# The mixing's two diagonal blocks as 64-row matmuls into two banks, with the work around it reordered

## The reference, cut to what matters

```python
# x: (32, 64, 1024); two layers, each: x = x + ffn(cond(x, c))
def L0_cond(x, c, weight, c_weight, bias):      # grouped conv, 4 groups, 9 taps, + context per (n, o)
    out = conv_general_dilated(x, weight, padding=[(4, 4)], feature_group_count=4)
    return out + (c @ c_weight.T)[:, :, None] + bias[None, :, None]
def L0_ffn(x, weight, bias, lora_A, lora_B, starts):   # x @ weight.T (1024 x 1024) + bias + adapter of rank 16
    ...
def L1_cond(x, emb, W0, b0, W1, b1, W2, b2, weight, bias_k):
    h = gelu(emb @ W0 + b0); h = gelu(h @ W1 + b1); att = softmax(h @ W2 + b2)   # (32, 8)
    agg_w = einsum('bk,koi->boi', att, weight[..., 0])                            # one 64 x 64 per batch row
    agg_b = att @ bias_k
    return einsum('boi,bih->boh', agg_w, x) + agg_b[:, :, None]                   # "the mixing"
def L1_ffn(x, A, B, Wr):                          # 64 adapters of rank 16, 16 of them chosen per token
    scores = xf @ Wr.T; top_vals, top_idx = top_k(scores, 16); gates = softmax(top_vals)
    h = einsum('nd,krd->nkr', xf, A)              # 1024 x 1024
    return 2.0 * einsum('nkr,kdr->nd', h * G[:, :, None], B)                      # 1024 x 1024
```

## Time and profile before

| what | us |
|---|---|
| median of three runs | 669.21 |
| the profiled execution's own time | 671.31 |
| its span, first to last instruction | 669.5 |
| PE busy | 651.7 |
| PEld busy | 538.4 |
| DVE busy | 451.1 |
| ACT busy | 213.1 |
| POOL busy | 73.2 |

### The profile page before, as it was taken

One profiled execution on the slowest core, in us unless ns is written; L12 is line 12 of the kernel. 1 busy time (PEld: TensorE's weight loads), 2 busy tenths in 40 slices (PEclk: granted clock), 3 DMA queues, 4 the chain that ended last, 5 costly groups with the idle time before them and its releaser, 6 DMA issues.

```text
span 669.5 us, 8350 instructions
## 1 busy us (share of the span) xinstructions
PE 651.7 (97%) x3197; PEld 538.4 (80%) x3197; DVE 451.1 (67%) x688; ACT 213.1 (32%) x275; POOL 73.2 (11%) x91
## 2 busy tenths in 40 slices
PE   9999999997999999999999999999899999999996
PEld 7878888886897787887789788888689888888775
DVE  2859469549377788658669648636867847656864
ACT  2714134224134115335114312334323321333510
POOL 1499200000000070000000042000000000000000
PEclk9999999998999999999999999999999999999999
DMA  8577715976968836776985682374987664047684
GB/s 306 189 293 277 288 48 160 353 218 216 381 222 317 349 148 253 261 233 234 338 305 186 273 314 94 107 225 157 348 316 266 270 258 162 0 140 206 227 318 182
DMA packets 51450, 157.98 MB, mean 236 GB/s; under 512 B 5472, under 2 KB 6368, under 8 KB 51424
## 3 DMA queue, kind: packets, MB, share of 16 engines
q1 hardware_dynamic: 46096, 148.05, 60.6%
q10 hardware_dynamic: 5328, 9.61, 4.7%
HBM read 131.94 MB, written 25.71 MB: 235 GB/s over the span
## 4 chain that ended last, share of the span: by engine, by line
PE 59%; DMA 19%; DVE 14%; issue 3%; ACT 3%; ACTq 1%; SPq 0%; DVEq 0%
PE bank L1349 14%; PE bank L1351 13%; PE bank L1350 13%; DMA gate_x<-gates 12%; PE bank L1363 8%; DMA piece_lo<-kept 4%; PE bank L1383 3%; DMA raw<-pieces 3%; DVE piece_lo L882 2%; PE bank L1370 2%; ACT piece_hi L639 2%; DVE work L977 1%; DVE x L914 1%; DMA toep<-taps 1%; PE bank L1375 1%
## 5 line engine op out<-in xcount | busy, mean ns | idle before, releaser
L882 DVE TENSOR_TENSOR piece_lo<-raw,piece_hi 128x1024 fp32r<-128x1024 f32 x60 | 74.1, 1240 | 89.9 <-ACT piece_hi L639 89.7
L1349 PE MATMUL bank<-piece_hi,u_hi 128*128 128x512 f32 x272 | 109.0, 401 | 8.1 <-DVE piece_lo L882 4.6
L639 ACT ACTIVATE piece_hi<-raw 128x1024 fp32r<-128x1024 f32 x60 | 63.3, 1057 | 155.0 <-PE bank L1351 110.6
L1350 PE MATMUL bank<-piece_lo,u_hi 128*128 128x512 f32 x272 | 107.9, 397 | 0.0
L1351 PE MATMUL bank<-piece_hi,u_lo 128*128 128x512 f32 x272 | 107.8, 396 | 0.0
L1349 PE MATMUL bank<-v_hi,piece_hi 128*128 128x512 f32 x256 | 101.8, 398 | 0.0
L1351 PE MATMUL bank<-v_hi,piece_lo 128*128 128x512 f32 x256 | 101.1, 395 | 0.0
L1350 PE MATMUL bank<-v_lo,piece_hi 128*128 128x512 f32 x256 | 101.0, 394 | 0.0
L1349 PE MATMUL bank<-piece_hi,v_hi 128*128 128x512 f32 x192 | 76.2, 397 | 1.3 <-DMA piece_lo<-kept 1.3
L1351 PE MATMUL bank<-piece_hi,v_lo 128*128 128x512 f32 x192 | 75.8, 395 | 0.0
L1350 PE MATMUL bank<-piece_lo,v_hi 128*128 128x512 f32 x192 | 75.7, 394 | 0.0
(11 more groups left out here) (143 smaller groups left out, 800.2 us busy)
## 6 DMA issues: line engine op xcount, KB each, us to landing
raw<-pieces SPq DMA_DIRECT2D x76, 512.0 KB, 5.3
piece_hi<-kept SPq DMA_DIRECT2D x48, 512.0 KB, 4.9
piece_lo<-kept SPq DMA_DIRECT2D x48, 512.0 KB, 5.8
conv_in<-conv_x SPq DMA_DIRECT2D x16, 516.0 KB, 6.9
x<-x SPq DMA_DIRECT2D x16, 512.0 KB, 5.3
gate_x<-gates ACTq DMA_DIRECT2D x32, 256.0 KB
out<-x SPq DMA_DIRECT2D x32, 256.0 KB, 4.6
conv_in<-pieces SPq DMA_DIRECT2D x12, 512.0 KB, 8.7
```

What stands on the lines that cost most here:

```text
L639: act.activation(piece_hi[:, n % SLOTS, :], raw[:, r % RAWS, :], ACT.Copy).then_inc(s_piece_hi, 1)
L882: dve.tensor_tensor(piece_lo[:, n % SLOTS, :], raw[:, r % RAWS, :], piece_hi[:, n % SLOTS, :].bitcast(F32), ALU.subtract).then_inc(s_piece ...
L1349: pe.matmul(to, left_hi, right_hi, start=first, stop=False)
L1350: pe.matmul(to, left_hi, right_lo, start=False, stop=False)
```

## The change

It does eight things.

1. `mix` makes two matmuls per tile in place of one: partitions 0 to 63 with the first diagonal block, 64 to 127 with the second, 64 moving columns each. The first goes to bank `first`, the second to bank `first + 1`, in columns `t * 64` on. So a chunk has eight matmuls of 64 rows, and fills half of each of two banks. All banks are now one tensor, so that `mix_item` reads both halves in one instruction.
2. `LAG` goes from 3 to 2; the mixes use two pairs of banks (2 and 3, 5 and 6 in group 0; 6 and 7, 3 and 4 later). `h` of chunk 1 moves to bank 1 and the transposed scores to bank 0.
3. In groups 1 to 3 the mixes 0 and 1 are issued ahead of the last quarter of `winograd(12, ...)`, and on DVE their items and low parts ahead of four `x1` adds. The adds of banks 4 and 5 go ahead of those of 6 and 7.
4. In group 1 the splits of combined unit 3 leave the mixing: two go ahead of `choose`, two behind `split_raw(g, 17)`; SP's `keep_weights(3, ...)` and `load_conv_in` move later with them.
5. In group 0 `split_first(20)` and `split_first(21)` go into the middle of `combine(2)` and its splits.
6. `split_raw(g, 25)` goes ahead of `sums(4)`.
7. In the last group the `partial` of the last product is added into `x1` ahead of time, and its banks 1 and 0 are added straight into `x1`; the stores' counts follow.
8. `score_transposed` and the waits are renumbered to match.

```diff
-LAG = 3
+LAG = 2
-        H_BANKS = (2, 3, 6, 7, 4, 5, 2, 3)
+        H_BANKS = (2, 1, 6, 7, 4, 5, 2, 3)
+        FIRST_MIX_BANKS = (2, 5)
+        MIX_BANKS = (6, 3)
...
-            def mix(c, bank):
+            def mix(c, first):
                 for t in range(NT):
-                    mm = pe.matmul(banks[bank][:, t * P:(t + 1) * P], x1[:, t, c * P:(c + 1) * P],
-                                   blockdiag[:, t, :], start=True, stop=True)
+                    for b in range(2):
+                        rows = slice(b * C, (b + 1) * C)
+                        mm = pe.matmul(bank[:, first + b, t * C:(t + 1) * C], x1[rows, t, c * P:(c + 1) * P],
+                                       blockdiag[rows, t, rows], start=True, stop=True)
                 mm.then_inc(s_mix, 1)
...
-                winograd(12, (1, 0), u_hi, u_lo, block_of(1, 1), False)
+                winograd(12, (1, 0), u_hi, u_lo, block_of(1, 1), False, range(3))
+                pe.wait_ge(s_bd, 2 * g + 2)
+                pe.wait_ge(s_f, g * 24 + 20)
+                for i in range(LAG):
+                    mix(CHUNKS[i], MIX_BANKS[i])
+                winograd(12, (1, 0), u_hi, u_lo, block_of(1, 1), False, range(3, 4))
...
@@ DVE, group 0
-                combine(2)
-                for step in range(4):
-                    combined_lo(2, step)
-                for n in range(20, 23):
-                    split_first(n)
+                combine(2, 0)
+                split_first(20)
+                combine(2, 1)
+                combined_lo(2, 0)
+                combined_lo(2, 1)
+                split_first(21)
+                combined_lo(2, 2)
+                combined_lo(2, 3)
+                split_first(22)
...
@@ DVE, groups 1 to 3, at the mixing
+                for i in range(2):
+                    mix_item(g, i, CHUNKS[i], MIX_BANKS[i])
+                for i in range(2):
+                    mix_lo(g, i, CHUNKS[i])
+                for s in range(2):
+                    add(partial[:, s, :], 2 + s, 0, s_f)
+                for s in range(2):
+                    ffn_done(7 + s)
+                    read(s_f, 21 + s)
+                    add(banks[1 - s][:, :], 2 + s, 0, s_f)
+                for i in range(2, NCH):
+                    mix_item(g, i, CHUNKS[i], MIX_BANKS[i % 2])
+                    if i > 2:
                         mix_lo(g, i - 1, CHUNKS[i - 1])
-                    if g == 1 and i % 2:
-                        combined_lo(3, i // 2)
...
+                split_raw(g, 25)
                 dve.wait_ge(s_lo, g * ITEMS + ITEMS)
                 sums(4)
-                split_raw(g, 25)
...
+                if last:
+                    for s in range(2):
+                        for h in range(2):
+                            add(partial[:, s, :], 2 + s, h, s_o)
+                    for s in range(2):
+                        won(dve, g, 1, 6, s)
+                        for h in range(2):
+                            read(s_o, 17 + 2 * s + h)
+                            add(banks[1 - s][:, :], 2 + s, h, s_o)
```

More of the change, by code:

```diff
@@ L150, in adaln_ffn_kernel @@
         diag = x1[0:C, 2, 0:GB * C].rearrange("p (b c) -> p b c", b=GB)
-        banks = [ctx.enter_context(nc.psum_tensor(f"bank{i}", [P, HALF], F32)) for i in range(8)]
+        bank = ctx.enter_context(nc.psum_tensor("bank", [P, 8, HALF], F32))
+        banks = [bank[:, i, :] for i in range(8)]
         s_first = sem("s_first")
@@ L495, in group @@
                 next_raw(17)
-                if g == 1:
-                    for step in range(4):
-                        keep_weights(3, step)
-                elif not last:
+                if g > 1 and not last:
                     load_conv_in(g + 1, 0)
@@ L503, in group @@
                 if g == 1:
-                    load_conv_in(g + 1, 0)
-                    load_conv_in(g + 1, 1)
-                if not last:
+                    keep_weights(3, 0)
+                    keep_weights(3, 1)
+                elif not last:
                     load_conv_in(g + 1, 2)
                     load_conv_in(g + 1, 3)
-                for n in range(19, 22):
-                    next_raw(n)
+                next_raw(19)
+                if g == 1:
+                    keep_weights(3, 2)
+                    keep_weights(3, 3)
+                next_raw(20)
+                next_raw(21)
                 if not last:
@@ L515, in group @@
                 next_raw(23)
+                if g == 1:
+                    for t in range(NT):
+                        load_conv_in(g + 1, t)
                 if g == 1:
@@ L917, in add_partial, with mix_item @@
                 dve.tensor_tensor(partial[:, s, :], partial[:, s, :], banks[bank][:, :], ALU.add).then_inc(done, 1)
[L919 removed]
+            def mix_item(g, i, c, first):
                 dve.wait_ge(s_mix, g * NCH + i + 1)
[L921 to L922 removed]
+                dve.tensor_tensor(work[:, c, :].rearrange("p (t b c) -> p b t c", b=2, c=C),
+                                  bank[:, first:first + 2, 0:HALF // 2].rearrange("p b (t c) -> p b t c", c=C),
+                                  mixb_bc[:, :, :].rearrange("p (t b) c -> p b t c", b=2), ALU.add).then_inc(s_item, 1)
             def mix_lo(g, i, c):
@@ L1245, in group @@
                 for s in range(2):
-                    add(partial[:, s, :], 2 + s, 0, s_f)
+                    ffn_done(5 + s)
+                    read(s_f, 15 + s)
+                    add(banks[4 + s][:, :], 2 + s, 1, s_f)
                 for s in range(2):
@@ L1327, in group @@
                     split_raw(g, STEPS + 2)
[L1328 to L1333, removed]
+                if last:
[7 more added lines that the diff above has]
+                            add(banks[1 - s][:, :], 2 + s, h, s_o)
+                else:
+                    for s in range(2):
+                        won(dve, g, 1, 6, s)
+                        add_partial(1 - s, s, s_o)
+                        read(s_o, 17 + 3 * s)
+                        add(partial[:, s, :], 2 + s, 0, s_o)
+                        add(partial[:, s, :], 2 + s, 1, s_o)
             first_group()
@@ L1582, in sum_of, with winograd @@
                     return lambda part, k, s: part[:, 2 * i + k // 2, (2 * (k % 2) + s) * P:(2 * (k % 2) + s + 1) * P]
-                def winograd(n, to, hi, lo, rows, stop):
-                    for j in range(2):
-                        if n + j in RAW:
+                def winograd(n, to, hi, lo, rows, stop, parts=range(4)):
+                    for part in parts:
+                        j, s = part // 2, part % 2
+                        if s == 0 and n + j in RAW:
                             raw_ready(n + j)
-                        else:
+                        elif s == 0:
                             fetched(n + j)
[L1591 to L1597, removed]
+                        for c in range(2):
+                            k = 2 * j + c
+                            mm = product(banks[to[s]][:, :], rows(hi, k, s), rows(lo, k, s),
+                                         *columns_piece(n + j, c), k == 0, stop and k == 3)
+                        if part:
+                            mm.then_inc(s_win, 1)
                 def sum_ready(step):
```

83 lines of the change are left out of this document (42 added, 41 removed).

## The result

| | us | runs |
|---|---|---|
| before | 669.82 (666.76 to 673.29) | 4 |
| after | 688.87 (687.29 to 694.26) | 4 |
| ratio | 1.030, 95% interval 1.022 to 1.037 | |

The change makes the kernel 3% slower: +19 us where -6 was forecast, and outside the range. Executions in which the granted clock was clearly lower than in the others of the same kernel are left out of all comparisons; this concerns two of the four of experiment 4 alone (716.46 and 717.14 us).

What follows compares the result with a forecast made beforehand. PE bounds the kernel, busy 651.7 of 669.5 us. Stalls and group 1's mixing give -11.8, switching +5.4, together -6.4: 669.2 becomes 662.8 us, 657 to 669 by the switch's bounds; the 8-in-10 range is 644 to 671.

Steps and rivals of the forecast that it cites:

- piece 20, piece 25, the end: PE's stalls on late DVE splits in group 0 (4.7 us) and groups 1 to 3 (4.9), and DVE's last adds (1.3), go.
- group 1's splits, keeps, conv loads (part 4): Group 1's mixing falls from 17.60 to group 2's 16.74 us, 0.9 gained; later conv loads and keeps cost nothing.
- stream of a chunk: A chunk's mix records on PE: loads side by side in two halves, 0.89 us as before; bounds 0.45 to 1.78.
- switch, 27 blocks: PE turning from 128 rows to 64 and back around each mix block: 0.2 us each, 5.4 in all; bounds 0 to 11.3.
- LAG 2 and the hoisted mixes: Low parts take DVE 1.4 us within at least 1.6, no wait but close; hoisted mixes 0 and 1 covered by 0.8.
- rival C: Stalls come back elsewhere, PE waiting for gate_x or kept pieces; half of 11.8 us lost, 669 us; chance 0.14.
- Rival A: Mix halves stream side by side and loads do not bound; mixes save 14.1 us, 643 to 655, about 649; chance 0.36.
- Rival B: Loads of the two halves go one at a time; a chunk's mix costs 1.78 us, +28.5, 691 us (686 to 697); chance 0.10.
- the clock's recovery after piece 20: Group 0: thirteen matmuls after PE's stall took 4.2 us in place of 3.0 at 1.2 GHz; 1.2 us gained.

Runs made afterwards that it cites:

- experiment 4: Kernel after, with a chunk's four matmuls of the first half issued before the four of the second; 703.95 and 704.55 us in two runs.
- experiment 5: Kernel before, with only parts 5, 6 and 7 of the change (pieces 20, 21 and 25 split earlier, last adds); 659.94 us, ratio 0.983.
- experiment 1: Kernel after with part 4 undone: group 1's unit 3 splits, keeps and conv loads in their old places; 675.56 us, ratio 1.007.
- experiment 2: Kernel after, with 128-row mixes again, four matmuls a chunk into the first bank of each pair; 674.98 us, ratio 1.003.
- experiment 3: Kernel after with both 128-row mixes and part 4 undone; LAG 2, hoisted mixes and parts 5 to 7 stay; 663.68 us, ratio 0.987.
- experiment 6: Experiment 3 with seventy-two 512-column matmuls of h in the loop body each made as two of 256 columns; 670.29 us, ratio 0.998.
- experiment 8: Experiment 3 with LAG 3, three single mix banks and three mixes hoisted in place of two; 660.53 us, ratio 0.984.
- experiment 9: Kernel after, with group 1's four conv loads issued later, behind raw piece 33, keeps staying where the change puts them; 684.61 us, ratio 1.019.
- experiment 10: Experiment 1 with group 1's four conv loads left late, behind raw piece 23, keeps and splits in their old places; 686.60 us, ratio 1.024.

## Why the prediction was wrong

The terms, by its own steps:

| step | predicted | measured | from |
|---|---|---|---|
| piece 20, piece 25, the end | -10.9 | -10.8 | experiment 5 |
| group 1's splits, keeps, conv loads (part 4) | -0.9 | +11.3 to +13.3 | experiments 1 to 3 |
| stream of a chunk | 0.89 us, unchanged | 0.89 us | turn after |
| switch, 27 blocks | +5.4 (0.20 each) | +9.5 (0.35 each) | turns, experiment 2 |
| loop body longer by 128 PE records | not seen | +2.6 | waits after; experiment 6 |
| LAG 2 and the hoisted mixes | 0, "no wait, but close" | +0.5 (+1.6 to +2.4 with 128-row mixes and part 4 undone) | waits after; experiments 3, 5, 8 |

With 12.3, the middle of part 4's two values, -10.8 + 12.3 + 9.5 + 2.6 + 0.5 = +14.1, against +16.9 between the profiled spans and +19.1 between the medians, whose interval is 5 us to either side. The last 3 to 5 us I can't place.

- **The step that failed** is in part 4: "SP's later conv loads and keeps serve a conv some 60 us on, also nothing." It asked only whether the moved transfers arrive in time for those who use them. They do. It did not ask what they land beside. Part 4 costs 11.3 to 13.3 us where it was forecast to give 0.9, and the place of the conv loads alone makes 4.7 to 7.3 of that (experiments 9 and 10). The stretch they moved into holds the raw pieces 18 to 23 and the eight spreads of `gate_x`, DVE's gated items wait for these, and PE waits for the last of them. The row for the slack was even at hand: rival C counted 0.9 us of it in group 2, and 4 MB of writes and 2 MB of loads were set against such a slack at no price. The other half of this step, two low parts ahead of the gates, was priced at 2.3 us without cover; the gates did leave 1.8 us later (280.32 against 278.51), and what it cost was not measured by itself. The 0.9 us of the mixing itself did come: after, group 1's turns are as long as group 2's.
- **The switch** had the right mechanism and bounds of 0 to 0.42 us a block. I took the middle, 0.20, on the ground that the rows at the upper end carried waits for semaphores. It is 0.35, near the upper bound, so the term was 4.1 us too small. The prediction said that the Trainium skill ("TensorEngine Tiling (Array Packing)", Key Properties), with its rule that a change of the tiling mode drains the engine, would put the sum near the upper end; the trace agrees, at 0.35 us for the way there and back.
- **The stream** came out as argued. Within a half a record of 64 moving columns starts every 0.112 us, as one of 128 rows and 128 columns does, so halving the moving columns gained nothing. Both still load 128 columns, which fits the reading that the load sets the pace; no run here varies the load by itself. Rival A, beside which stood the Trainium skill's speedup of up to 2x ("TensorEngine Tiling (Array Packing)", Theoretical Speedup), gets no support here: the stream of a chunk is 0.89 us before and after. That tiles of one mode load and multiply in parallel, the second part of the Trainium skill's rule ("TensorEngine Tiling (Array Packing)", Key Properties), the trace bears out: 0.056 us a record on the average with the halves in alternation.
- **Rival B** gave 691 and the time came near that, but its mechanism (a chunk of 1.78 us) is refuted by the chunk of 0.89. The agreement is an accident.
- **Rival C** named the right victim, `gate_x`, but for another reason (PE earlier at the gates) and at half the stalls' gain. That a moved transfer could be the cause was in none of the rivals, which is why the range stopped at 671.
- **The stalls** of DVE's order were together worth what their rows said, 10.8 us against 10.9, the clock's recovery after piece 20 among them: from 150 to 170 us the granted clock after is 1.00. The last DVE operation now starts nearer the last matmul: from PE's last start to the span's end it is 686.4 - 682.08 = 4.3 us, before 669.5 - 663.94 = 5.6, so 1.3 as forecast.

## What to carry to other kernels

When a transfer is moved, list what else is in flight in its new stretch and who waits for that; the question whether it arrives in time for its own reader is the easier half. Count the microseconds of a matmul by its loads as well as by its columns, and count the change from 128-row to 64-row matmuls and back as a price of its own; many short blocks of 64 rows pay it each time. And read a wait's releaser with doubt where the engine named had done the same work before without a wait: here the wait went with the size of a loop's body.

## What the hardware showed that was not expected

- A block of 64-row matmuls among 128-row ones costs 0.35 us for the two changes (turn 2.40 against 2.05 us), with no wait shown for it on PE; its first load isn't made ahead (426.84, with the first matmul), while 112- and 113-row matmuls among those of 128 rows stay 0.23 us apart.
- 64-row float32 records with 64 moving columns start 0.112 us apart within a half, as 128-row ones with 128 columns do. With the halves in alternation two series run side by side (0.056 us on the average); with eight of one half ahead of eight of the other the second series starts 0.50 us behind the first, before that ends (0.089).
- With 777 matmul records in a round of PE's loop (group 2 before) the instruction queue brings 13 packets, with 840 and with 849 it brings 32, and the first matmul of the second and third round then stands for 1.05 to 1.80 us, put down to DVE.
- Eight spreads of 256 KB and two megabytes of loads issued within 0.3 us of the fifth spread: the loads land after 13.5 us in the median instead of 6.8, and DVE's waits for the spreads go from 2.3 to 9.7 us.
